# A state-space stage in which one PSUM bank feeds the next chunks: its fills dealt out over the steps, ScalarE's reads of them half a step apart

## The reference, cut to what matters

```python
x = x + ssm(layernorm(x))
# ssm, with B=2 sequences of L=2048 tokens, 512 inner channels, 16 states
xz = einsum('bld,ed->ble', x, W_in);  x_ssm, z = split(xz, 2)
xc = silu(causal_dwconv(x_ssm, conv_w, conv_b))          # 4 taps
dt_raw, B_vals, C_vals = split(einsum('bld,ed->ble', xc, W_x))
dt = softplus(dt_raw * dt_w + dt_b)
h_t = exp(dt * A) * h_(t-1) + dt * B_t * xc              # per channel and state
y_t = sum over the states of h_t * C_t  + xc * D_param
y = y * silu(z);  out = einsum('bld,ed->ble', y, W_out)
```

## Time and profile before

| | |
|---|---|
| median of 3 runs | 3145.12 us (3144.73 to 3145.34) |
| the profiled execution | 3123.03 us, its span 3121.1 us |
| SSM stage in the span | about 0 to 1042 us |
| DVE busy, whole span | 2463.4 us (79%) |
| PE busy, whole span | 2852.5 us (91%) |
| ACT busy, whole span | 1960.9 us (63%) |
| POOL busy, whole span | 1033.3 us (33%) |

### The profile page before, as it was taken

How to read it: one execution, slowest core, us unless ns; L and a number is a source line. 1 busy time by engine, 2 the same in 40 slices (tenths; PEclk the granted TensorE clock), 3 DMA queues, 4 the chain that set the end, 5 groups by cost and what they waited for, 6 DMA issues and landing times. The chain is left out here.

```text
span 3121.1 us, 48071 instructions
## 1 busy us (share of the span) xinstructions
PE 2852.5 (91%) x14250; PEld 1222.2 (39%) x14251; DVE 2463.4 (79%) x2883; ACT 1960.9 (63%) x3568; POOL 1033.3 (33%) x507
## 2 busy tenths in 40 slices
PE   8899899889877878999999999999999998499998
PEld 3334334334323431222222222222222226499997
DVE  4999999999999668888888888888888845344443
ACT  4765765656644335788787787878788785244443
POOL 4878879779774130000000000000000003522222
PEclk9999999999989987999999999999999998699999
DMA  2111111111111452111101111111101104633332
GB/s 69 34 51 55 40 52 58 35 54 51 34 51 47 132 178 41 32 42 42 40 23 33 41 42 42 39 35 42 42 25 33 37 1 146 219 50 48 48 49 36
DMA packets 125209, 169.40 MB, mean 54 GB/s; under 512 B 25552, under 2 KB 87760, under 8 KB 125008
## 3 DMA queue, kind: packets, MB, share of 16 engines
q1 hardware_dynamic: 110992, 148.19, 16.9%
q0 software_dynamic: 13440, 18.16, 3.5%
q10 hardware_dynamic: 576, 0.55, 0.1%
HBM read 125.80 MB, written 40.74 MB: 53 GB/s over the span
## 5 line engine op out<-in xcount | busy, mean ns | idle before, releaser
L1742 DVE TENSOR_REDUCE nmh<-ring 128x2 f32<-128x1024 f32 x1024 | 1196.0, 1219 | 180.1 <-PE ring L1619 179.7
L1600 ACT ACTIVATE prob<-s_ps 128x512 f32<-128x512 f32 x2048 | 1073.1, 603 | 283.0 <-PE s_ps L1640 282.9
L879 DVE TENSOR_TENSOR_SCAN h<-dA,state,bx 128x512 f32<-128x512 f32 x512 | 618.5, 1265 | 32.1 <-ACT dA L673 31.7
L413 POOL TENSOR_TENSOR bx<-u,bb 128x2048 f32<-128x2048 f32 x127 | 574.4, 4528 | 193.1 <-DVE h L879 193.1
L1640 PE MATMUL s_ps<-qs,ks 98*128 98x512 bf16 x2048 | 613.7, 387 | 17.6 <-issue 11.9
L1652 PE MATMUL acc<-prob,vst 128*32 128x512 f32 x4096 | 549.3, 608 | 0.2 <-ACT prob L1600 0.2
L673 ACT ACTIVATE dA<-dt,aneg 128x512 f32<-128x512 f32 x512 | 348.5, 691 | 270.8 <-DVE h L879 267.7
L742 PE MATMUL y_ps<-h,ident 128*128 128x512 f32 x1024 | 492.6, 626 | 0.0
L1640 PEld LDWEIGHTS s_ps<-qs,ks 98*128 98x128 bf16 x2048 | 149.3, 97 | 580.6 <-ACT prob L1600 475.1
L1619 PE MATMUL ring<-k,q 64*128 64x512 bf16 x2048 | 347.9, 395 | 27.8 <-DVE nmh L1742 19.6
L742 PEld LDWEIGHTS y_ps<-h,ident 128*128 128x128 f32 x1024 | 207.2, 202 | 232.8 <-issue 226.8
(11 more groups left out here) (253 smaller groups left out, 2486.9 us busy)
## 6 DMA issues: line engine op xcount, KB each, us to landing
bb<-b_rows SPq DMA_DIRECT2D x128, 256.0 KB, 3.1
q<-parts SPq DMA_DIRECT2D x256, 64.0 KB, 2.1
parts<-part SPq DMA_DIRECT2D x48, 256.0 KB, 2.5
qs<-parts SPq DMA_DIRECT2D x192, 64.0 KB, 2.8
ks<-parts SPq DMA_DIRECT2D x192, 64.0 KB, 2.9
xt<-slots_in SPq DMA_DIRECT2D x72, 133.0 KB, 2.1
k<-parts SPq DMA_DIRECT2D x256, 32.0 KB, 2.0
fo<-in_x SPq DMA_DIRECT2D x8, 512.0 KB, 4.3
```

The costliest lines, as they stand in the source:

```text
L413: nc.gpsimd.tensor_tensor(bx[:, n % BR], u[:, b], bb[:, n % RB, None, :].to_broadcast([P, KI, CH]), ALU.mult).then_inc(s_bx, 1)
L879: nc.vector.tensor_tensor_scan(h[:, n % HR, d, :], dA[:, d % 2, :], bx[:, n % BR, d, :], state[:, b, n, d:d + 1], ALU.mult, ALU.add).then_ ...
L1600: nc.scalar.activation(prob[:, k % PR, j, :], s_ps[:, tile % SR, :], ACT.Exp, scale=SC).then_inc(s_exp, 1)
L1742: nc.vector.tensor_reduce(nmh[:, slot, t, 2 * s:2 * s + 2], ring[:, s, :, :], AX.X, ALU.max, negate=True).then_inc(s_free[s], 1)
```

## The change: what it does

TensorE's `side` deals its fills out otherwise: Z as 1, 2, 1 over steps 7, 8, 9; T in steps 9 and 10; E as 1, 2, 1 over steps 10, 11, 12; V in steps 13, 14, 15 and, as before, 0. ScalarE reads the first fill of a step in `between` of the next step, and the second in its own `side`. The softplus instructions are dealt out two at a time over `side(3)`, `between(4)`, `side(4)`, `between(5)`. In chunk 0, z is projected in steps 5 and 6, read in `side(5)` to `between(7)`, and its SiLU, with two table loads of its own, is in `side(14)`. `xT0` now lies in `xres`. The counts of `s_free` follow.

```diff
-        xT0 = h[:, HR - 1, 0:KM, :]
+        xT0 = xres[:, :, :].rearrange("p t e -> p (t e)").rearrange("p (k l) -> p k l", k=KM)
...
-            def softplus_in(c, b, half):
+            def softplus_in(c, b, d):
                 wait(act, s_full, fill_dt(c) + 1)
...
             def between(i, b, n, has_next):
-                if known(c, 0) and n == 1:
-                    take_z(0, 0, 2)
-                    take_z(0, 0, 3)
+                if n == 0 and has_next and not known(c, 0):
+                    take_conv(c + 1, 1 - b, 2)
                 if n == 1 and has_next:
                     take_conv(c + 1, 1 - b, 3)
...
-                if n == 8 and has_next:
-                    take_z(c + 1, 1 - b, 1)
-                if n == 9 and has_next:
-                    take_z(c + 1, 1 - b, 3)
+                if n in (4, 5) and has_next:
+                    softplus_in(c + 1, 1 - b, 2 * n - 7)
+                if known(c, 0) and n in (6, 7):
+                    take_z(0, 0, 2 * n - 11)
+                if n in (8, 9) and has_next:
+                    take_z(c + 1, 1 - b, 2 * n - 16)
                 if two:
                     if n == 10:
-                        take_xT(c + 2, 1)
+                        take_xT(c + 2, 0)
                     if n == 11:
-                        take_conv_in(c + 2, 1)
+                        place_halo(c + 2, b)
+                        take_conv_in(c + 2, 0)
                     if n == 12:
+                        take_conv_in(c + 2, 2)
+                    if n == 13:
                         take_conv_in(c + 2, 3)
-                    if n in (13, 14, 15):
-                        take_conv(c + 2, b, n - 13)
+                    if n in (14, 15):
+                        take_conv(c + 2, b, n - 14)
             def side(i, b, n, has_next):          # ScalarE
-                    take_z(0, 0, 0)
-                    take_z(0, 0, 1)
...
-                    silu_z(c, b)
+                    if not known(c, 0):
+                        silu_z(c, b)
+                    power_tables()
+                if known(c, 0) and n == 14:
+                    silu_z(0, 0)
                     power_tables()
...
+                if known(c, 0) and n in (5, 6):
+                    take_z(0, 0, 2 * n - 10)
...
+                if n in (8, 9) and has_next:
+                    take_z(c + 1, 1 - b, 2 * n - 15)
                 if two:
                     if n == 10:
-                        place_halo(c + 2, b)
-                        take_conv_in(c + 2, 0)
+                        take_xT(c + 2, 1)
                     if n == 11:
-                        take_conv_in(c + 2, 2)
+                        take_conv_in(c + 2, 1)
             def side(i, b, n, has_prev, has_next):          # TensorE
                 if known(c, 0) and n == 0:
-                    for d in range(KI):
-                        project_in(0, KI + d)
                     pe.wait_ge(s_pa, 7)
+                if known(c, 0) and n in (5, 6):
+                    project_in(0, KI + 2 * n - 10)
+                    project_in(0, KI + 2 * n - 9)
...
```

More of the change, by code:

```diff
@@ L179, in ssm_stage @@
         NW = 2
-        FIRST = KI
+        FIRST = 0
         EACH = 18
@@ L190, in base @@
                 return base(NC - 2) + 9
-            return EACH * c + FIRST - 2
+            return EACH * c + KI - 2
         def after_out(c):
-            return 3 if known(c, 0) else 5
+            return 3 + KI if known(c, 0) else 5
         PF_T0, PF_E0, PF_V0, PF_T1 = 0, KM, KM + KI, KM + 2 * KI
@@ L227, in fill_Z @@
             if known(c, 0):
-                return d
+                return 3 + d
             return base(c - 1) + after_out(c - 1) + d
@@ L492, in third_part @@
                 nc.scalar.copy(parts[64:64 + NR, b, :], r1[:, :]).then_inc(s_p2, 1)
-            def softplus_in(c, b, half):
+            def softplus_in(c, b, d):
                 wait(act, s_full, fill_dt(c) + 1)
-                for d in (2 * half, 2 * half + 1):
-                    nc.scalar.activation(tA[:, d, :], fill[:, :], ACT.Abs,
-                                         bias=dtb[:, d:d + 1], scale=dtw[:, d:d + 1]).then_inc(s_abs, 1)
-                    last = nc.scalar.activation(dt[:, b, d, :], fill[:, :], ACT.Relu,
-                                                bias=dtb[:, d:d + 1], scale=dtw[:, d:d + 1])
-                if half:
+                nc.scalar.activation(tA[:, d, :], fill[:, :], ACT.Abs,
+                                     bias=dtb[:, d:d + 1], scale=dtw[:, d:d + 1]).then_inc(s_abs, 1)
+                last = nc.scalar.activation(dt[:, b, d, :], fill[:, :], ACT.Relu,
+                                            bias=dtb[:, d:d + 1], scale=dtw[:, d:d + 1])
+                if d == KI - 1:
                     last.then_inc(s_free, 1)
@@ L634, in side @@
                     root(c + 2)
-                if n == 3 and has_next:
-                    softplus_in(c + 1, 1 - b, 0)
-                if n == 4 and has_next:
-                    softplus_in(c + 1, 1 - b, 1)
+                if n in (3, 4) and has_next:
+                    softplus_in(c + 1, 1 - b, 2 * n - 6)
+                if known(c, 0) and n in (5, 6):
+                    take_z(0, 0, 2 * n - 10)
                 if n == 5 and has_next:
@@ L645, in side @@
                     softplus_minus(c + 1)
-                    take_z(c + 1, 1 - b, 0)
                 if n == 8 and has_next:
                     softplus_ln(c + 1, 1 - b)
-                    take_z(c + 1, 1 - b, 2)
-                if n == 9:
-                    if has_next:
-                        third_part(c + 1, 1 - b)
-                    if two:
-                        take_xT(c + 2, 0)
+                if n == 9 and has_next:
+                    third_part(c + 1, 1 - b)
+                if n in (8, 9) and has_next:
+                    take_z(c + 1, 1 - b, 2 * n - 15)
                 if two:
                     if n == 10:
-                        place_halo(c + 2, b)
-                        take_conv_in(c + 2, 0)
+                        take_xT(c + 2, 1)
                     if n == 11:
-                        take_conv_in(c + 2, 2)
+                        take_conv_in(c + 2, 1)
             def chunk(i, b, has_prev, has_next):
@@ L819, in side @@
                     project_out(c - 1, 1 - b, n - 5)
-                if n in (7, 8) and has_next:
-                    project_in(c + 1, KI + 2 * n - 14)
-                    project_in(c + 1, KI + 2 * n - 13)
+                if n == 7 and has_next:
+                    project_in(c + 1, KI)
+                if n == 8 and has_next:
+                    project_in(c + 1, KI + 1)
+                    project_in(c + 1, KI + 2)
+                if n == 9 and has_next:
+                    project_in(c + 1, KI + 3)
                 if two:
@@ L825, in side @@
                         transposes(c + 2, 0)
+                    if n == 10:
                         transposes(c + 2, 1)
-                    if n in (10, 11):
-                        project_in(c + 2, 2 * n - 20)
-                        project_in(c + 2, 2 * n - 19)
-                    if n in (12, 13, 14):
-                        convolve(c + 2, n - 12)
+                        project_in(c + 2, 0)
+                    if n == 11:
+                        project_in(c + 2, 1)
+                        project_in(c + 2, 2)
+                    if n == 12:
+                        project_in(c + 2, 3)
+                    if n in (13, 14, 15):
+                        convolve(c + 2, n - 13)
             def chunk(i, b, has_prev, has_next):
```

## The result

The changed kernel takes 3125.43 us (median of 7 runs, 3119.89 to 3128.32), the kernel before 3144.73 in runs beside them (3134.98 to 3146.14): ratio 0.9937, 95% interval [0.9928, 0.9947]. The forecast was 3125, a ratio of 0.9936. In a later set of runs, where the kernel before takes 3123.68, the changed kernel takes 3105.46, ratio 0.9944 [0.9928, 0.9961]. The change is therefore a small gain, clear of noise in both sets.

The account below looks back on a forecast made before the run. VectorE's train of steps bounds the SSM stage, with TensorE's list setting each middle chunk's second half. Chunk 0's 7.9, the middle chunks' 8.5 and chunk 6's 3.8 make 20.2 us off 3145.12: 3125, range 3113 to 3138 (8 of 10).

Parts of the forecast that it names:

- The head: Chunk 0's start: convolution no longer behind four Z, so step 2 starts at 74.4 against 85.50, 11.1 us earlier.
- Given back in chunk 0: New VectorE stalls in chunk 0 from step 2 on: 2.6 + 2.3 + 0.4 + 1.4 = 6.7 us, against 3.5 before.
- Step 6's 2.6: Chunk 0, stall for dA ahead of step 6: 2.6 us, with step 4's collect at half clock making Z0 late.
- TensorE's list has a head start here, so it sets nothing: Chunk 0: no residual for Z0 to wait for, so TensorE's list adds no term to the sum.
- rival E: Chunk 0, `side(14)`: each of two table switches costs more than its load, 2.6 us more, 3128 (5%).
- A middle chunk: Chunks 1 to 5: a stall of 0.67 and a handoff of 1.03 go, 1.70 us each, 8.5 in all.
- rival D: Slower: the half clock gets into TensorE's list, two steps in each of six chunks, 30 us, 3155 (5%).
- Chunk 6: Stalls for dA shrink or go, including 0.99 ahead of step 2: 3.8 us less, bounds 1.9 to 4.6.
- Rival A: Chunks 1 to 6: TensorE's list doesn't bind, VectorE's stalls all go, 22 us plus chunk 0's 7.9, 3115 (12%).
- B: Handoff Z1 to Z2 longer, Z1 read behind `u<-xs`: list 0.9 longer, 9 us gained in all, 3136 (15%).
- C: Chunk 0 alone gains, and is eaten: B plus half clock through steps 5 and 6, about 4 us, 3141 (8%).
- the 22 us between timed and profiled execution: Whole kernel: median of runs 22.09 above the profiled execution, carried over unchanged to the forecast time.

Follow-up runs that it names:

- first profile: Profiled execution of the changed kernel, unaltered, from the first set of runs, against the kernel before: 3125.43 us, ratio 0.9937.
- second profile: Profiled execution of the changed kernel, unaltered, from the later set of runs, against the kernel before: 3105.46 us, ratio 0.9944.

## Why the prediction was right, and where its steps were not

**The head, 11.1 us less.** Right. In the first profile the convolution starts at 63.81, the second bx holds step 1 by 2.02, step 2 starts at 76.08; with the first scan 1.78 later than before these are 62.0 and 74.3, forecast 62 and 74.4. GpSimd now sets the start of step 1, as worked out.

```profile
63.81 3.60 PE L704 MATMUL fill<-xs,taps 128*128 128x512 f32 x8
...
67.44 2.46 DVE L889 TENSOR_TENSOR_SCAN h<-dA,state,bx 128x512 f32<-128x512 f32 x2 [2.02 <-POOL bx L413]
...
76.08 2.46 DVE L889 TENSOR_TENSOR_SCAN h<-dA,state,bx 128x512 f32<-128x512 f32 x2
```

**Given back in chunk 0: 6.7 forecast, 6.2 measured (0.48 + 2.17 + 2.03 + 1.54), for partly wrong reasons.** The stalls, first profile of the changed kernel:

```profile
104.25 2.46 DVE L889 TENSOR_TENSOR_SCAN h<-dA,state,bx 128x512 f32<-128x512 f32 x2 [0.48 <-ACT dA L674]
113.43 2.46 DVE L889 TENSOR_TENSOR_SCAN h<-dA,state,bx 128x512 f32<-128x512 f32 x2 [2.17 <-ACT dA L674]
136.26 2.46 DVE L889 TENSOR_TENSOR_SCAN h<-dA,state,bx 128x512 f32<-128x512 f32 x2 [2.03 <-POOL bx L413]
172.39 2.46 DVE L889 TENSOR_TENSOR_SCAN h<-dA,state,bx 128x512 f32<-128x512 f32 x2 [1.54 <-ACT dA L674]
```

Step 7's 2.3 and step 15's 1.4 came out (2.17, 1.54). Step 6's 2.6 rested on the low clock in step 4's collect, and that collect took 3.60, though TensorE idled 3.07 ahead of it: the stall is 0.48. In its place came the third, ahead of step 10, where 0.4 was forecast: 2.03 in the first profile, 0.34 in the second. The first profile's 8.5 for chunk 0 is thus near the forecast's 7.9 by luck; the second's 10.2 is the forecast's upper bound, 9.9 for the full clock in step 4. The step that failed is "TensorE's list has a head start here, so it sets nothing". The head start is what makes the handoff Z1 to Z2 long (4.05 us for 2.55), and with the low clock behind it the list does hold VectorE, for 2.03.

**The table loads of `side(14)`** (rival E). Each takes 1.28 with the next instruction at its end, and the stall is 1.54, not 4.1. The Trainium skill (ScalarE: Activation LUTs, What ACT_TABLE_LOAD costs) puts a switch at 2.66 us with a drain counted in; here no drain shows between the rows, and the measurement decides.

```profile
167.05 1.28 ACT L477 ACT_TABLE_LOAD   x1
168.35 1.91 ACT L477 ACTIVATE zs<-zs 128x2048 f32<-128x2048 f32 x1
170.28 1.28 ACT L436 ACT_TABLE_LOAD   x1
171.57 1.30 ACT L674 ACTIVATE dA<-dt,aneg 128x512 f32<-128x512 f32 x2
```

**A middle chunk, 1.70 less.** Right where O1 runs at full clock (1.7 to 2.0), and its signs came out: no stall ahead of step 4, 0.65 ahead of step 10 (0.6), the list 68.76 us (68.8) at clock 1.00. The gate waits 1.53 instead of 1.1. Mis-sized is the sum over five chunks, 6.4 for 8.5 (6.5 in the second profile): two chunks lose 1.3 each to O1 at the low clock. The forecast had the low clock as rival D, inside the list, and didn't look at what stands ahead of it, although show it at step 4. The edit left 2.47 us of idling ahead of O1 in the chunks that were hit, where the kernel before had 0.4 to 2.0 in its middle chunks. With matmuls of zeros in the idle places the toll is gone in all ten middle chunks.

**Chunk 6**: 4.3 in the first profile for 3.8, but 3.0 in the second, where the stall ahead of step 2 came back with 1.19; the forecast had let it go. **Rival A** falls: the gates of chunks 1 to 5 wait for y_ps. **B** is right as a mechanism wherever TensorE leads: in chunk 0, and with the residuals moved. **C's** sum is slightly off: by B's own terms it is 4.5 - 1.2 + 1.9 = 5.2, not 4.

So the mechanism was right in the main, but that the total was right to 0.5 us is partly luck. The stage gave 17.3 to 17.5 us and not 20.2, while the medians differ by 19.3 in the first set and 18.2 in the second. And the 22 us between timed and profiled execution, which the forecast carried over, did not carry over: 3144.73 to 3123.03 before, 3125.43 to 3123.07 after. The two ratios, 0.9937 and 0.9944, are what the change is worth.

## What to carry to other kernels

Where TensorE idles a few microseconds in a steady loop, look at which instruction behind the idling is short of time: here the low clock fell on one that VectorE waits for in some turns of the loop and on others in the rest. A few matmuls that add zeros, in the idle places, took the toll away here and made no chunk longer. An engine that is given a head start can arrive in front of a reader that is still busy, and idle there: move the reader with it. Where a view names a releaser, count which one of its instructions the code waits for at that point. One profile of a kernel is not its time: take a second one before explaining a difference of one or two microseconds. And when a span doesn't move, compare the stage that was changed, not the whole.

## What the runs showed of the hardware

- The low clock came from execution to execution in other chunks: in the changed kernel the waits for C behind a slow O1 stood at 353.57, 472.77 and 941.49 in the first profile, at 350.35, 705.34 and 940.83 in the second. In a middle chunk each cost 1.07 us in VectorE's wait and made the chunk 1.3 us longer.
- Idling of 3.07 us on TensorE ahead of step 4 was followed by the low clock in some chunks of the changed kernel (5.29 and 6.30 for the collect's 3.60) and not in others (3.60, also in chunk 0). O1 behind 2.47 us of idling was slow in chunks 2 and 3 of the first profile, and ran at full clock in chunk 3 of the second. What went with it in 40 middle chunks was the skip part some 39 us earlier: O1 slow where it had taken 3.70, full where it had taken 5.28 to 5.40. Why, no run here tells.
- The scatter of 64 row groups took 80.0 to 81.0 us in twelve profiled executions and 99.3 in one, with the gaps in GpSimd's waits for `g` and for `row_in`.
